# A mixture-of-experts layer's loop over the experts, closed by each tile count's own program instead of by a shared end

## What is computed

```python
logits = xf @ router_w.T                       # 8 experts, each token goes to its best 2
top_v, top_i = jax.lax.top_k(logits, 2)
C = ceil(T * 2 * 1.25 / 8)                     # 1280 slots for each expert, T = 4096
xb = buf[:E * C].reshape(E, C, D)              # the rows of the tokens that an expert was given
gu = jnp.einsum('ecd,efd->ecf', xb, w12)       # 512 -> 2 x 2048
h = jax.nn.silu(g) * u
yb = jnp.einsum('ecf,edf->ecd', h, w3)         # 2048 -> 512
out = jnp.zeros((T, D)).at[tokens].add(yb * weight)
x = x + tanh(g_ffn) * out
```

## Time and profile before

| | us |
|---|---|
| median of 3 runs | 2902.11 (2899.45 to 2902.37) |
| the profiled execution, its own time | 2903.15 |
| its span, first to last instruction | 2901.4 |
| PE busy | 2691.8 (93%) |
| DVE busy | 1399.5 (48%) |
| ACT busy | 982.7 (34%) |
| POOL busy | 412.7 (14%) |
| mean granted TensorE clock | 0.962 |

### The profile page before, as it was taken

How to read it: one execution, slowest core, us unless ns; L and a number is a source line. 1 busy time by engine, 2 the same in 40 slices (tenths; PEclk the granted TensorE clock), 3 DMA queues, 4 the chain that set the end, 5 groups by cost and what they waited for, 6 DMA issues and landing times.

```text
span 2901.4 us, 41353 instructions
## 1 busy us (share of the span) xinstructions
PE 2691.8 (93%) x14486; PEld 2418.3 (83%) x14487; DVE 1399.5 (48%) x2725; ACT 982.7 (34%) x2543; POOL 412.7 (14%) x393
## 2 busy tenths in 40 slices
PE   6999999759998999989999799989999899979977
PEld 5888888659997888868888688878888799979967
DVE  5777777534443434434443344434444344435545
ACT  4766766322223222222222322222223222233333
POOL 3455454310001000020000200010001100030020
PEclk8999999869999999999999899999999999989989
DMA  7522221222113111041111321131112311132232
GB/s 249 199 73 93 83 80 64 73 113 81 43 43 77 60 44 43 22 82 59 44 43 43 61 81 65 44 84 46 43 43 62 77 44 43 44 68 111 74 111 76
DMA packets 60135, 209.49 MB, mean 72 GB/s; under 512 B 9564, under 2 KB 9836, under 8 KB 51602
## 3 DMA queue, kind: packets, MB, share of 16 engines
q1 hardware_dynamic: 43282, 175.30, 16.8%
q0 software_dynamic: 16640, 31.69, 5.8%
HBM read 145.60 MB, written 67.70 MB: 74 GB/s over the span
## 4 chain that ended last, share of the span: by engine, by line
PE 72%; issue 4%; DVE 1%; ACT 1%; DMA 0%; DVEq 0%; POOL 0%; ACTq 0%; POOLq 0%
PE bank L1364 72%; PE bank L1370 1%; DVE yacc L1303 1%; DVE slotsT_lo L1271 0%; ACT slotsT_hi L1185 0%; DMA raw<-in_moe_w_dram 0%; DVE h L1323 0%; DVE w_lo L1258 0%; ACT w_hi L1181 0%; POOL out_dram L1161 0%; DVE w_lo L1265 0%; ACT h_hi L1226 0%; ACT yout L1212 0%; DVEq L1302 0%; DVEq L1269 0%
## 5 line engine op out<-in xcount | busy, mean ns | idle before, releaser
L1364 PE MATMUL bank<-slotsT_hi,w_hi 128*128 128x384 f32 (+2 forms) x2560 | 892.5, 349 | 104.4 <-issue 101.2
L1364 PE MATMUL bank<-slotsT_lo,w_hi 128*128 128x384 f32 (+2 forms) x2560 | 888.9, 347 | 0.0
L1364 PE MATMUL bank<-slotsT_hi,w_lo 128*128 128x384 f32 (+2 forms) x2560 | 886.7, 346 | 0.0
L1364 PEld LDWEIGHTS bank<-slotsT_hi,w_hi 128*128 128x128 f32 x2560 | 486.1, 190 | 137.1 <-issue 104.8
L1323 DVE TENSOR_TENSOR h<-silu,bank 128x384 f32<-128x384 f32 (+2 forms) x320 | 183.7, 574 | 844.3 <-PE bank L1364 843.2
L1364 PEld LDWEIGHTS bank<-slotsT_lo,w_hi 128*128 128x128 f32 x2560 | 486.5, 190 | 25.1
L1364 PEld LDWEIGHTS bank<-slotsT_hi,w_lo 128*128 128x128 f32 x2560 | 485.9, 190 | 22.3
L1226 ACT CAST h_hi<-h 128x384 fp32r<-128x384 f32 (+2 forms) x320 | 169.3, 529 | 749.3 <-DVE h L1323 749.3
L1220 ACT ACTIVATE silu<-bank 128x384 f32<-128x384 f32 (+2 forms) x320 | 162.0, 506 | 755.5 <-PE bank L1364 755.1
L1364 PE MATMUL bank<-w_hi,h_hi 128*128 128x512 f32 x1008 | 401.2, 398 | 7.1 <-DVE yacc L1303 7.1
L1303 DVE TENSOR_TENSOR yacc<-bank,yacc 128x512 f32<-128x512 f32 x464 | 317.8, 688 | 183.7 <-PE bank L1364 176.0
(11 more groups left out here) (158 smaller groups left out, 2922.0 us busy)
## 6 DMA issues: line engine op xcount, KB each, us to landing
raw<-in_moe_w_dram SPq DMA_DIRECT2D x65, 1536.0 KB, 6.2
xrow<-expert_rows SPq DMA_DIRECT2D x42, 520.0 KB, 9.2
expert_rows<-zeros SPq DMA_DIRECT2D x40, 520.0 KB, 7.8
xin<-in_x_dram SPq DMA_DIRECT2D x16, 512.0 KB, 3.7
xres<-in_x_dram SPq DMA_DIRECT2D x16, 512.0 KB, 3.7
out_dram<-xres SPq DMA_DIRECT2D x16, 512.0 KB, 3.5
probs<-in_L_xattn_Wq_dram SPq DMA_DIRECT2D x1, 1024.0 KB, 10.6
probs<-in_L_xattn_Wo_dram SPq DMA_DIRECT2D x1, 1024.0 KB, 6.8
```

Source lines behind the costliest of these rows:

```text
L1364: last = nc.tensor.matmul(out_ap, st, mv, start=(at == 0), stop=(at == n - 1))
```

## The change

PE, ACT and DVE loop over the experts by labels. The count is tested by compare-and-branch instructions with the programs in the same order as before. Each program ends with the loop's own closing: it raises the index, and a compare-and-branch leads straight back to the load of the next count. For this branch a prefetch hint stands ahead of the program's last chunk. When no expert is left, a jump leads to the end.

```diff
             def experts(eng, chunk):
-                with eng.Fori(0, E) as e:
+                mine = [eng.engine]
+                name = f"experts_{len(loops)}"
+                loops.append(name)
+                top, end = f"{name}_top", f"{name}_end"
+                index = nc.alloc_registers(f"{name}_i", engines=mine)
+                nc.regs_mov(index, 0)
+                nc.br(top, engines=mine)
+                with nc.body(top, valid_engines=mine):
+                    e = nc.snap(index, min_val=0, max_val=E - 1)
                     n_e = eng.value_load(counts[0:1, bass.ds(e, 1)], min_val=0, max_val=T)
 
                     def whole(nt):
...
                                 chunk(nt, e, pair * 2 + i, i % 2, pair + 1, False, False)
+                        here = eng.mark_branch_hint_location()
                         chunk(nt, e, NCH - 1, (NCH - 1) % 2, NCH // 2, False, True)
-
-                    by_tiles(eng, n_e, whole)
+                        nc.regs_alu(index, index, 1, op=ALU.add)
+                        left = f"{name}_{nt}_left"
+                        eng.br_lt(index, E, on_true=top, on_false=left).branch_hint(here)
+                        with nc.body(left, valid_engines=mine):
+                            nc.br(end, engines=mine)
+
+                    def pick(sizes):
+
+                        if len(sizes) == 1:
+                            whole(sizes[0])
+                            return
+                        more = f"{name}_over_{sizes[0]}"
+                        eng.br_lt(n_e, sizes[0] * P + 1, on_true=f"{name}_{sizes[0]}", on_false=more)
+                        with nc.body(more, valid_engines=mine):
+                            pick(sizes[1:])
+
+                    pick(TILES)
+                    for nt in reversed(TILES[:-1]):
+                        with nc.body(f"{name}_{nt}", valid_engines=mine):
+                            whole(nt)
+                nc.switch_bb(end)
+
+            loops = []
```

## The result

The kernel with the change takes 2813.2 us, the median of four runs (2812.6 to 2817.3), against 2902.2 for the kernel before on the same chip: a ratio of 0.97, 95% interval 0.9685 to 0.9714. The direction was right and the size too small.

The account below looks back on a forecast made before the run. PE bounds the kernel, busy 93% of the span; only its issue time in seven gaps can be won. 94.4 - 7 x 5.37 = 56.8 us off 2903.15 gives 2846.3, median 2845, with other terms 0; range 2828 to 2878.

Parts of the forecast that it names:

- the seven gaps: PE's idle issue time where one expert ends and the next begins: 94.4 us, 13.5 each, all the change can win.
- Part 4: Added hints and the last jump to the end: cost 0, with 2.4 us as the bound for the hints.
- Parts 1 and 2: At each expert's end, the jump to the common end and the jump back go, each priced at 3.8 us.
- Part 3: Count load, tests and third far jump stay: 5.37 us per gap, so 94.4 - 7 x 5.37 = 56.8 us won.
- the first entry: PE's way into the first expert, without the first two jumps: 6.73 us idle, 5.37 in the chain.
- third far jump: After the tests, the jump to the picked program's code, assumed to stay in every gap.
- the low end of its range: 2828 us: no third jump in three gaps, 3 us more each, and the clock in part.
- The second way to the sum: Check of the gain in the gaps from two jumps at 3.8 us each: 7 x 2 x 3.8 = 53 us.
- Part 5: Low clock after a gap, about 2.1 us each: 0 won; gaps under 3.0 us would win it, 15 at most.
- Part 6: Other engines at expert entries: ACT has 5.4 us to spare and must win 2.7; DVE, POOL and SP don't bind.
- the case that a hint brings nothing: Rival at the jump back: only dropping the jump to the end counts, 23 to 30 us, 2875; chance 0.28.

Follow-up runs that it names:

- the longer lead: The changed kernel with the last two tiles' sums of each last chunk in u's free banks, so PE's sequencer reaches the branch sooner: 2798.7 us.

## Why the prediction was wrong

**The place was right, and that both jumps go.** The change acts on the seven gaps and on nothing else. The jump to the end is gone and the jump back is short, the matmuls are the same in number, and DVE's busy time moved by 1.6 us. Part 4's costs of nothing hold: an expert without a gap begins 0.3 us behind the old one's last matmul, with the hint and the closing in between. (Part 4 spoke of three programs; there are eight, and five of them run.)

**Parts 1 and 2, the price of a jump: mis-sized.** They priced it at 3.8 us, from the starts of packets, 27 us for seven. By their own rows the seven jumps to the end took 31.0 us, 4.4 each, and the seven jumps back 43.9, 6.3 each, of which 1.9 are left. As runs, closing the loop in each program brought 37 us and the hint 50. The starts of the packets are a bad clock for this: between the first two, 3.3 and 4.3 us apart, I had put one whole jump, and the jump back alone takes 6.1. The rows of the branches themselves, 3.3 to 5.1 and 6.1 to 6.9, were in the trace before, and the 2.4 us of lead with them. Why the jump back from the far end is dearer stays open (with a hint of its own, on the old loop, it took 4.2); that it follows another far jump is not the reason, since behind a hinted one it still took 5.7.

**Part 3, "What stays": the step that failed.** It took the first entry's 5.37 us as what stays of every gap, with a third far jump in each, and multiplied it by seven. The measured rest is 4.64 + 4.32 + 4.15 and, at the other four, 0.54 + 0.31 + 0.24 + 0.32, 14.5 us instead of 37.6. These 23 us are the whole of what the issue time lacked (94.4 - 14.5 = 79.9 against 56.8). The first entry holds a jump of 6.08 us into a program whose code has never been run. Four of the seven gaps have no such jump: three times the program behind the tests is picked, and once the one for 9 tiles behind an expert of 10, by a jump of 0.34 us. The row that would have shown it is the kernel before's own, the tests at the first gap (window 925:945):

```profile
L1071 PEldq COMPARE_BRANCH  x7: 65/65/80, 940.4 to 943.3; - x7
```

Each of the seven tests takes 80 ns at the most, and the first matmul follows at 943.6 (930.22 and 13.38): no third jump, where the forecast assumed one in each gap. It was so before the change already: line 1071 has a far jump into a program in three of the seven gaps (3.5, 4.1 and 4.5 us), as the change has. What the tests do have is a hole of 2.2 us between the fourth and the fifth, so the third packet of the earlier trace rows, which the forecast gave to the third jump, is rather that of a straight run into a block that isn't there. Five gaps have such a hole, 10.1 us in all. In the change it is gone with the jumps. The text named this case for the low end of its range ("the largest program, which lies directly behind the tests and may need no third jump in three of the seven gaps"), with 3 us each, and it was worth 5 in four. The second way to the sum, 7 x 2 x 3.8 = 53, agreed with the first by luck: its price was too small and it left out the hole, while the first kept four jumps that aren't made.

**Part 5, the clock: 0 was wrong, its low bound was near.** It allowed that some gaps might get short enough to win their 2.1 us, and set this at an end of the range. Four did, and four times 2.1 is 8.4 of the 9.8 us by which the matmuls are shorter. Its 3.0 us at the full clock are one gap's figure and no rule: in the change's gap of 4.64 us the granted clock is 0.98, so it fell only at the very end.

**Part 6 held.** ACT has to shorten its route too, or PE waits: 2857.5 us measured against 2864 worked out. SP and POOL did not come into it.

**The sum, from the rows of both kernels.** In the seven gaps the jumps to the end bring 31.0 us, the jumps back 42.1 (43.9 - 1.9), the hole some 10; the jumps into the picked programs cost 1.2 more (12.5 to 13.7) and the loads of the count 2.5 (2.2 to 4.7). That makes 79, against the 79.9 of idle time. The first entry gives 0.8 back (6.73 to 7.55 us), which leaves the 79.1 of the waits, and with 9.8 for the matmuls it is 88.9 of the 89.5 us of the spans.

**The rule that was weighed.** The forecast gave 0.28 to the case that a hint brings nothing, beside the page of the Trainium skill "Runtime: NRT & Kernel Launch", section "Instruction fetch mechanics", with its two lines of code and purely sequential prefetch. On one point the trace agrees: a taken branch out of reach stalls, here for 3.3 to 6.9 us. On the other it doesn't: the hinted jump back takes 0.23 to 0.36 us, and an expert of 10 tiles runs without one packet of code. Where they differ the measurement decides.

## What to carry to other kernels

Time a branch by its own row in the trace before pricing a jump, and look at each place where it is taken: one program's entry may cost 6 us and its neighbour's nothing. In a loop whose body is larger than the engine's store of code, leave no far jump without a hint, and put the program that is picked most often right behind the tests (here 23 us between two orders of the same programs); who closes the loop matters little. Before changing one engine's route, ask which others take the same one: ACT's and DVE's was worth nothing alone and 44 us once PE's was short.

## What the runs showed of the hardware

- A far branch on PE took 3.3 to 6.9 us in the kernel before, most of all back from behind all the programs; some far ones took 0.2 to 0.4 us without a hint (9 tiles behind 10, the jump back behind the 5 tiles). In the change the hinted jump back took 0.23 to 0.36 us; a test that doesn't jump takes 65 ns.
- A hint given 170 to 340 us ahead works as well as one given 28 to 49 us ahead (2814.8 and 2813.2). Given a few instructions ahead it is too late for the jump (29.1 us in seven, without it 28.9), and still won 30 us, about half of it as a hole between the tests that closed. Given an expert ahead of a branch that a far jump leads to, it left the jump at 3.6 to 4.7 us.
- With every jump covered, PE went 365 us, one expert of 10 tiles and its closing, without a code packet; with one jump uncovered a like stretch had 8, with two 10.
- Behind a gap of 4.6 us the granted clock was 0.68 for 5 us, behind a gap of 0.3 us 1.00.

Hinting the third jump, into the picked program, wasn't tried. It is what is left of the gaps: three of 4.2 to 4.6 us, some 13 us in all, and 5.6 us with the longer lead.
